# Attention's beginning: modulation as rows that are turned, its second set and the gates behind the first scores, the first stack head by head

## The reference, cut to what matters

```python
mod = (_silu(L0_c) @ L0_wmod).reshape(L0_c.shape[0], 6, 1, -1)      # 8 x 3072 in six parts of 512
sa, ca, ga, sb, cb, gb = (mod[:, 0], ..., mod[:, 5])
ga = (2 * (ga >= 0) - 1) * jnp.maximum(jnp.abs(ga), 0.25)           # gb the same
h = _layernorm(x, axis=-1) * (1 + ca) + sa
x = x + ga * attention(h)            # 16 heads of 32, causal, T = 512, 8 batches
h = _layernorm(x, axis=-1) * (1 + cb) + sb
x = x + gb * mlp(h)                  # 512 -> 1024 -> 1024 -> 512
```

## Time and profile before

| | us |
|---|---|
| median of 3 runs | 1564.84 |
| lowest and highest | 1563.7, 1569.16 |
| the profiled execution | 1568.6 |
| its span, first to last instruction | 1566.8 |
| PE busy in it | 1457.9 (93%) |
| first scores start in it | 55.78 |
| fourth slot (p = 3) starts in it | 94.47 |

### The profile page before, as it was taken

One profiled execution on the slowest core, in us unless ns is written; L12 is line 12 of the kernel. 1 busy time (PEld: TensorE's weight loads), 2 busy tenths in 40 slices (PEclk: granted clock), 3 DMA queues, 4 the chain that ended last, 5 costly groups with the idle time before them and its releaser, 6 DMA issues.

```text
span 1566.8 us, 30447 instructions
## 1 busy us (share of the span) xinstructions
PE 1457.9 (93%) x12112; PEld 1321.2 (84%) x12112; DVE 1110.3 (71%) x1957; ACT 809.5 (52%) x1462; POOL 439.1 (28%) x451
## 2 busy tenths in 40 slices
PE   7989999999999999994699999969999999989998
PEld 6678888788878888873599999969999999989998
DVE  4477877777777777672676676686676666778887
ACT  3156666666676667673355555555243333353331
POOL 2156566656576666672000000000000000000000
PEclk9889999999999999996899999999999999999999
DMA  6534435343434343435344444543665555688885
GB/s 215 161 83 122 97 93 125 86 122 74 123 88 118 94 123 88 95 73 180 122 142 142 141 143 169 214 148 113 238 229 209 209 202 203 219 283 268 284 291 179
DMA packets 126590, 247.16 MB, mean 158 GB/s; under 512 B 13672, under 2 KB 36200, under 8 KB 126448
## 3 DMA queue, kind: packets, MB, share of 16 engines
q1 hardware_dynamic: 122816, 242.57, 49.6%
q10 hardware_dynamic: 3632, 2.64, 0.5%
HBM read 114.58 MB, written 79.72 MB: 124 GB/s over the span
## 4 chain that ended last, share of the span: by engine, by line
PE 42%; DVE 6%; DMA 3%; ACT 2%; issue 1%; DVEq 0%; SPq 0%; ACTq 0%
PE sum_b L2111 11%; PE sum_e L2111 7%; PE sum_a L2111 7%; PE aux L2051 6%; PE sum_b L2107 5%; PE sum_e L2107 3%; PE sum_a L2107 2%; DMA y_dram<-u_c 1%; PE aux L2061 1%; DVE op L1683 1%; DMA gate_mlp_row<-gate_dram 1%; PE aux L2039 1%; DVE w L1819 1%; DVE u_c L1736 1%; DMA x_dram<-x_rows 1%
## 5 line engine op out<-in xcount | busy, mean ns | idle before, releaser
L429 POOL TENSOR_TENSOR prob_lo<-prob,prob_hi 128x512 f16<-128x512 f32 x256 | 296.9, 1164 | 141.6 <-ACT prob L533 141.1
L526 ACT ACTIVATE prob_hi<-key_score 128x512 f16<-128x512 f32 x320 | 191.2, 597 | 132.0 <-PE key_score L824 129.8
L2111 PE MATMUL sum_b<-op,w 128*128 128x256 f32 x1728 | 222.7, 288 | 13.6 <-DVE op L1683 9.8
L2111 PEld LDWEIGHTS sum_b<-op,w 128*128 128x128 f32 x1728 | 216.0, 195 | 16.2 <-issue 11.3
L735 PE MATMUL lin<-h_parts,wqkv 128*128 128x512 f32 x768 | 220.4, 411 | 1.1 <-DVE h_parts L578 1.1
L533 ACT ACTIVATE prob<-key_score 128x512 f32<-128x512 f32 x320 | 190.7, 596 | 0.0
L697 DVE TENSOR_REDUCE row_max<-score 128x1 f32<-128x512 f32 (+2 forms) x384 | 180.6, 499 | 13.5 <-PE score L811 12.7
L735 PEld LDWEIGHTS lin<-h_parts,wqkv 128*128 128x128 f32 x768 | 144.4, 197 | 30.5 <-DVE h_parts L578 2.9
L811 PE MATMUL score<-stack 96*128 96x512 f32 (+3 forms) x512 | 155.6, 365 | 0.0
L2111 PE MATMUL sum_e<-op,w 128*128 128x256 f32 x1152 | 148.1, 286 | 2.7 <-DVE w L1819 2.7
L2111 PE MATMUL sum_a<-op,w 128*128 128x256 f32 x1152 | 145.4, 284 | 2.3 <-issue 2.3
(11 more groups left out here) (153 smaller groups left out, 2574.1 us busy)
## 6 DMA issues: line engine op xcount, KB each, us to landing
stack<-qk_parts SPq DMA_DIRECT2D x384, 128.0 KB, 2.4
late_op_whole<-y_dram SPq DMA_DIRECT2D x40, 512.0 KB, 4.9
y_dram<-u_c SPq DMA_DIRECT2D x32, 512.0 KB, 3.1
blk<-y_dram SPq DMA_DIRECT2D x32, 512.0 KB, 4.5
y_dram<-y_sum SPq DMA_DIRECT2D x24, 512.0 KB, 4.6
x_tiles<-x SPq DMA_DIRECT2D x32, 256.0 KB, 3.7
attn_dram<-o_rows SPq DMA_DIRECT2D x32, 256.0 KB, 2.3
attn_tiles<-attn_dram SPq DMA_DIRECT2D x8, 1024.0 KB, 6.2
```

What stands on the lines that cost most here:

```text
L429: nc.gpsimd.tensor_tensor(prob_lo[:, key[1] % 2, u, :], prob[:, u, :], prob_hi[:, key[1] % 2, u, :], ALU.subtract).then_inc(lo_pool, 1)
L526: nc.scalar.activation(prob_hi[:, q % 2, u, :], bank[:], ACT.Exp, scale=SOFTMAX_SCALE, bias=P_SHIFT)
L2111: mm = nc.tensor.matmul(dst, w[:, wl, c, cols], data[:, dl, c, :], start=begin, stop=end, skip_group_check=again)
```

## The change

1. The modulation is made as rows: `mod_rows(s)` has `silu` as weights (8 columns) and `wm` as 512 moving columns, four matmuls for each of shift and scale, into `key_bank`. ACT copies the rows to SBUF (`take_rows`), and `mod_columns(s)` turns them with four transposes each.
2. `mod_rows(1)` goes to slot 0, step 1, its turning to step 4. `gate_rows` go from slot 0 (steps 2 and 4) to slot 1 (steps 0 and 2). Their parts of `wmod` are loaded by ACT.
3. DVE's `take_gate` is gone. ACT copies the gate rows in slot 1 and POOL makes the gates at the start of slot 2 (`make_gate`, four operations each). PE's wait for the gates becomes one for ACT's copies; ACT's wait for the DMA stays.
4. For the first batch, turns 2 and 3 use the banks of the scores and places in `o_rows`, so the four turns need not wait for one another, and QK 0 and QK 1 are interleaved in PE's list, by rows of `h`.
5. `weights_high` and `weights_low` stand between the turns: one block before, one after turn 1, four after turn 3 (before: three and three).
6. The first stack is issued head by head, with a semaphore for each of the four heads. PE also still waits for `stack_in0`, which SP raises by its whole amount behind its twelfth issue.
7. POOL's constant rows of stacks 2 and 3 move to slot 1.

```diff
-    MOD_STEPS, GATE_STEPS = 2, 10
+    MOD_STEPS, GATE_STEPS = 2, 8
+    def turn_bank_of(n, c):
+        return score_bank[c - 2] if n == 0 and c >= 2 else lin_bank_of((TURN, c))
+    def full_of(n, c):
+        return o[:, c - 2].rearrange("p t n -> p (t n)") if n == 0 and c >= 2 else full[:, c % 2, :]
...
+                if n == 0 and g == 0:
                     for j in range(4):
+                        for block_row in range(3):
+                            load_rows(g, block_row, j, first_stack_in[j])
+                    sp.sem_inc(stack_in[0], 16 * STACK_DMAS)
+                    return
...
-            for step in (1, 2):
-                sp.wait_ge(mod_mm, step)
-                for half in range(2):
-                    load_mod(sp, 2 * step + half)
+            for half in range(2):
+                sp.wait_ge(mod_mm, half + 1)
+                load_mod(sp, 2 + half)
+            for item in before_first():
+                after_item(0, item)
...
+            def make_gate(g):
+                made = 4 * g
+                pool.wait_ge(gate_row, g + 1)
+                if g == 0:
+                    pool.wait_ge(mod_turned, 2)
+                nc.gpsimd.tensor_scalar(sign[:, g], gates[:, g], 0.0, 0.5, ALU.is_ge, ALU.subtract)\
+                    .then_inc(gate_step, 1)
+                pool.wait_ge(gate_step, made + 1)
+                nc.gpsimd.tensor_tensor(gates[:, g], gates[:, g], sign[:, g], ALU.mult).then_inc(gate_step, 1)
+                pool.wait_ge(gate_step, made + 2)
+                nc.gpsimd.tensor_scalar(gates[:, g], gates[:, g], GATE_FLOOR / 2, 4.0, ALU.max, ALU.mult)\
+                    .then_inc(gate_step, 1)
+                pool.wait_ge(gate_step, made + 3)
+                nc.gpsimd.tensor_tensor(gates[:, g], gates[:, g], sign[:, g], ALU.mult).then_inc(gate_step, 1)
             def slot(b, p, first, more):
+                if first and p == 2:
+                    for g in range(2):
+                        make_gate(g)
...
+            def take_rows(s):
+                for j in range(2):
+                    act.wait_ge(mod_mm, 2 * s + j + 1)
+                    nc.scalar.copy((gates, sign)[s][:, j], key_bank[j][0:B, :]).then_inc(mod_row, 1)
+            take_rows(0)
+            weights_high(0)
...
+                    if first and (p, u) == (0, 2):
+                        take_rows(1)
+                        for half in range(2):
+                            load_mod(act, 4 + half)
+                    if first and p == 1 and u in (1, 3):
+                        take_gate(u // 2)
...
             def do_item(n, item):
-                if item[0] == TURN or item[-1] == 0:
-                    place = ORDER.index(unit_of(item))
+                if n == 0 and item in (qk(0)[0], qk(1)[0]):
+                    pe.wait_ge(lin_taken, LIN_CREDITS + item[1] + 1)
+                elif (item[0] == TURN or item[-1] == 0) and not (n == 0 and item[0] == TURN):
                     pe.wait_ge(lin_taken, lin_no(n, unit_of(item)) + 1)
...
-            def mod_columns(s):
+            def mod_rows(s):
                 for j in (SHIFT, SCALE):
                     pe.wait_ge(wm_in[j], 16 * (s + 1))
-                    for block in range(NC_):
-                        at = ((s * 2 + j) * NC_ + block) * B
-                        for c in range(NC_):
-                            mm = nc.tensor.matmul(o_bank[:, at:at + B], wm[:, j, c, block * P:(block + 1) * P],
-                                                  silu[:, c, :], start=(c == 0), stop=(c == NC_ - 1))
-                mm.then_inc(mod_mm, 1)
+                    for c in range(NC_):
+                        mm = nc.tensor.matmul(key_bank[j][0:B, :], silu[:, c, :], wm[:, j, c, :],
+                                              start=(c == 0), stop=(c == NC_ - 1))
+                    mm.then_inc(mod_mm, 1)
...
+                        mm = nc.tensor.transpose(o_bank[:, at:at + B], rows[:, j, block * P:(block + 1) * P],
+                                                 ident[0:B, 0:B])
+            first_items[NC_:3 * NC_] = [item for pair in zip(qk(0), qk(1)) for item in pair]
...
                 if first and p == 2:
-                    pe.wait_ge(gate_step, GATE_STEPS)
-                    pe.wait_ge(ones_ready, 1 + GROUPS)
+                    pe.wait_ge(gate_row, 2)
+                    pe.wait_ge(ones_ready, 3)
...
-                    if first and p == 0 and u in (2, 4):
-                        gate_rows(u // 2 - 1)
+                    if first and (p, u) == (0, 1):
+                        mod_rows(1)
+                    if first and (p, u) == (0, 4):
+                        mod_columns(1)
+                    if first and p == 1 and u in (0, 2):
+                        gate_rows(u // 2)
```

More of the change, by code:

```diff
@@ L229, in attention @@
     stack_in = [mem.sem(f"stack_in{g}") for g in range(GROUPS)]
+    first_stack_in = [mem.sem(f"first_stack_in{j}") for j in range(4)]
     score_done, score_taken, max_hi, turn_done, turn_taken = (
@@ L347, in slot @@
                 for u in range(UNITS):
-                    if first and (p, u) == (1, 3):
+                    if first and (p, u) == (2, 0):
                         sp.wait_ge(gate_step, GATE_STEPS)
@@ L402, in low_part @@
                     pool.wait_ge(lin_taken, LIN_CREDITS + lin_no(n, item) + 1)
-                    nc.gpsimd.tensor_tensor(h[:, 1, c, :], full[:, c % 2, :], f32(h[:, 0, c, :]), ALU.subtract)\
+                    nc.gpsimd.tensor_tensor(h[:, 1, c, :], full_of(n, c), f32(h[:, 0, c, :]), ALU.subtract)\
                         .then_inc(h_low, 1)
@@ L418, in _ @@
             ones(1)
-            pool.wait_ge(w_lo, len(W_ORDER))
-            for g in range(GROUPS // 2, GROUPS):
-                ones(g)
-            pool.wait_ge(ones_ready, 1 + GROUPS)
-            def slot(b, p, first, more):
+            pool.wait_ge(ones_ready, 3)
+            def make_gate(g):
[12 more added lines that the diff above has]
+                nc.gpsimd.tensor_tensor(gates[:, g], gates[:, g], sign[:, g], ALU.mult).then_inc(gate_step, 1)
+            def slot(b, p, first, more):
+                if first and p == 2:
+                    for g in range(2):
+                        make_gate(g)
+                if first and p == 1:
+                    pool.wait_ge(w_lo, len(W_ORDER))
+                    pool.wait_ge(v_split, V_CREDITS + sum(item[0] == V and last_item(item)
+                                                          for item in before_first() + sum(WORK[0], [])))
+                    for g in range(GROUPS // 2, GROUPS):
+                        ones(g)
+                    pool.wait_ge(ones_ready, 1 + GROUPS)
                 for u in range(UNITS):
@@ L491, in after_item @@
                     act.wait_ge(stack_in[(g - 2) % GROUPS], 16 * STACK_DMAS * (n + 1 if g >= 2 else n))
+                    if n == 0 and g == 2:
+                        for j in range(4):
+                            act.wait_ge(first_stack_in[j], 16 * 3)
                 act.wait_ge(lin_done, lin_no(n, unit) + 1)
@@ L646, in _ @@
             normalise(0, range(NT))
-            for k in range(3):
-                weights_low(k)
             take_columns(0)
@@ L651, in _ @@
             take_mod(0)
+            weights_low(0)
             for item in before_first():
                 after_item(0, item)
+                if item == (TURN, 1):
+                    weights_low(1)
                 if item == (TURN, NC_ - 1):
-                    for k in range(3, len(W_ORDER)):
+                    for k in range(2, len(W_ORDER)):
                         weights_low(k)
-            take_columns(1)
             def gather_output(n, q, hh):
@@ L671, in slot @@
                 for u in range(UNITS):
-                    if first and p == 1 and u in (0, 2):
-                        take_gate(u // 2)
+                    if first and (p, u) == (1, 0):
+                        take_columns(1)
                     turned = behind(b, p, 1, first)
@@ L722, in turn @@
                     pe.wait_ge(x_norm, NT * (n + 1))
[L723 removed]
+                bank = turn_bank_of(n, c)
                 for t in range(NT):
@@ L780, in _ @@
             pe.sem_inc(pv_done, PV_CREDITS)
+            pe.wait_ge(pool_step, 8)
             pe.wait_ge(silu_step, 3)
+            mod_rows(0)
             mod_columns(0)
-            pe.wait_ge(pool_step, 8)
-            for item in before_first():
+            first_items = before_first()
+            first_items[NC_:3 * NC_] = [item for pair in zip(qk(0), qk(1)) for item in pair]
+            for item in first_items:
                 do_item(0, item)
-                if item == (QK, 1, NC_ - 1):
-                    pe.wait_ge(mod_taken, MOD_STEPS)
-                    mod_columns(1)
             def masks(b, p, u, key):
```

67 lines of the change are left out of this document (36 added, 31 removed).

## The result

| | before | after |
|---|---|---|
| median, both timed on the same chip (4 runs each) | 1565.44 | 1574.59 |
| lowest and highest after | | 1572.91, 1576.39 |
| the profiled execution and its span | 1568.6, 1566.8 | 1575.26, 1573.4 |
| first scores | 55.78 | 42.70 |
| slot 3 of the first batch | 94.47 | 98.18 |

The changed kernel takes 1.0051 times as long [1.0033, 1.0069]: slower by 0.5%. The forecast was 1562.1, 2.7 us faster, with a range that ended at 1568. Against the kernel before, 9.15 us more were measured by the two medians (8.0 by the ratio) where 2.7 less were expected.

The account below looks back on a forecast made before the run. PE was taken as drawn nearly without gaps, often at half clock. First scores 13.6 us earlier, then step (2, 2) almost 10 us late behind POOL's gates, left a 2.7 us gain: 1564.84 - 2.7 = 1562.1, range 1553.5 to 1568.

Parts of the forecast that it names:

- The path that it named: Slot 2, step (2, 2): PE waits for ACT's exponentials, gates_out and POOL's eight gate operations, opening at 84.0, almost 10 us late.
- mod_rows raise the clock: PE's start: mod_rows(0) runs half clock for 5.6 us, then full, ending at 18.9 instead of 22.73.
- That rival: Rows do not hold the clock: mod_rows run at half speed in the first stage and slot 0; 1572, chance 10%.
- The stage up to the first scores: First batch: QK 0 and 1 start at 24.2, first scores at 42.2, set by SP's twelve stack issues; 13.6 us earlier.
- The wait for the gates' wmod: PE ahead of the gate products: waits for ACT's late loads, bounds 0 and 3 us, taken as 1.0.
- The price of tensor_scalar on POOL: POOL's gate operations: 0.8 us per tensor_scalar, between 0.5 and 1.27, making the eight-operation chain 8.4 us.
- From gates to slot 3: POOL's chain ends at 80.1, gates_out lands at 82.7, step (2, 2) opens at 84.0, slot 3 at 91.8.
- What DVE gives back: Before slot 2, step 2: PE's 5.6 us wait for DVE's row maxima and 5.0 us of half clock go.
- "The rest is shifted as it is.": Behind slot 3 both instruction lists are the same, so the 2.7 us gain carries unchanged to the end.
- All is given back: Rival at step (2, 2): tensor_scalar at 1.27 and landing of 3.5 open it 2.9 us later still; 1565, chance 8%.
- Gates hidden: Rival on POOL: 0.3 us per operation on 8 partitions, slot 3 at 83.2, gain 11, 1553.6; chance 17%.
- the rival that I had set on that side: The slower side: rows of 8-column weights do not hold PE's clock, sum 10.0 us lost, 1572; chance 10%.

Follow-up runs that it names:

- rows_alone: The kernel before with only the modulation made as rows that are turned, slots, gates and stacks unchanged; ratio 0.9987 to the kernel before.
- all_mended: Changed kernel with gates on DVE, gates' wmod loads behind each row copy, no stack_in0 wait in batch 0, two weights_low later; 1554.34 us, ratio 0.9927.
- after_again: The changed kernel, unchanged, profiled a second time; span 1571.0 us.
- after_third: The changed kernel, unchanged, profiled a third time; span 1572.3 us.
- no_gate_math: Changed kernel with POOL's eight gate operations replaced by one signal, so the gates stay raw; ratio 0.9951 to the kernel before.
- gates_on_dve: Changed kernel with the gates made by DVE in three operations each, none on POOL; ratio 0.999 to the kernel before.
- gate_load_early: Changed kernel with ACT issuing each gates' part of wmod behind its own row copy, not behind both; ratio 1.001 to the kernel before.
- before_no_gate_math: The kernel before with each gate's five DVE operations replaced by one copy; ratio 0.9982 to the kernel before.
- gate_copy_ahead: all_mended with the second gate row copied at (1, 2), ahead of the row maxima's DMAs, and the second gate made at (1, 4); ratio 0.9938.
- pool_prices: no_gate_math with twelve extra POOL operations behind the last slot, results unused, to time them; one execution, 1574.51 us with the added work.
- before_third: The kernel before, unchanged, profiled a third time; span 1566.3 us.
- before_again: The kernel before, unchanged, profiled a second time; span 1563.1 us.

## Why the prediction was wrong

The path that it named held, and two prices on it did not: that of tensor_scalar on POOL, which turned the sign, and that of the wait for the gates' `wmod`. The sum put a gain of 13.6 us against a loss of 10.9 between the first scores and slot 3, a difference of two large numbers, and the loss was 16.8.

- **mod_rows raise the clock.** Right: 18.8 for 18.9. The second set took 7.03 for 7.0, at a clock of 1.00. That rival is out; rows_alone shows the same by itself (8.78 and 7.03). No row of the forecast shows that a load of 333 ns in the first 41 us is half clock, as it took for the size of the first QK pair and for the 0.11 us of a transpose; the 330 to 333 ns at 0.50 and 188 at 1.00 in the same trace, above, bear it out.
- **The stage up to the first scores.** Right to half a microsecond: QK 0 starts at 23.8 (24.2), QK 2 at 33.4 (33.6), first scores at 42.7 (42.2), released by SP behind its twelfth issue. The half clock in QK 0 and 1 was 3.4 us (24.9 to 28.3, at 0.50) and not 5.6, but DVE held QK 2 as the forecast said, for 1.84 us instead of 1.0, so the miss did not show. all_mended shows that this hold and `stack_in0` together cost 3.9 us.
- **The wait for the gates' wmod.** Taken at 1.0 of bounds 0 to 3: it was 2.2 in the profiled execution, inside, but by luck. In after_again and after_third it was 3.74 and 3.46, in no_gate_math and gates_on_dve 3.5, so the upper bound was too low. What I left out is what the wait does to the clock: it fell behind it (0.52 from 58.9 to 62.3), and the product took 5.30 for 3.60. Together 3.9 us, not 1.0 (in after_again 3.74 and 2.31, so 6.1). gate_load_early took 4.3 away at slot 3.
- **The price of tensor_scalar on POOL.** This is the step that failed. I took 0.8 and called 1.27 the upper bound, the price of a two-input operation, on the unstated assumption that one input cannot cost more than two. It costs 1.92. Four of them are 4.5 us beyond the forecast, the four tensor_tensor, at 1.25 to 1.28 for 1.2, and the signals 0.3, so the chain lasted 13.2 for 8.4. The row I leaned on was nearer than I let it be: the affine_select at 0.29 for 128 columns gives 1.2 for 512, and I took something off it. Between the engines, on 8x512 of the gates: a tensor_tensor takes 1.25 to 1.28 us on POOL (after) and 0.68 on DVE (before), a tensor_scalar with two operations 1.92 on POOL (after) and 0.39 on DVE (all_mended).
- **From gates to slot 3.** The chain began at 74.35 instead of 71.7, by the 0.5 us of the first scores and the 2.9 more for the wait, of which 2.65 reached it, and its write landed within 1.8 us instead of 2.5. Together: (2, 2) at 84.0 + 2.65 + 4.8 - 0.9 (0.7 of landing, the rest in the exponentials) = 90.5, as measured. From there to slot 3 it took 7.7 us, by the forecast 7.8.
- **What DVE gives back.** The 10.6 us of waits and half clock that before lost to DVE are gone in after, as forecast, but not for the reason given, that DVE's gate operations go: without them before_no_gate_math still waits 3.8 us for row maxima and gains 4.5 at slot 3. With the gates on DVE and PE as late as in after, gates_on_dve has no wait for row maxima; in all_mended, where PE opens slot 1 at 56.3 instead of 66.6, 1.3 us are back, and 3.8 in gate_copy_ahead. So it is argued, though no run tries it alone, that in after PE's own delay hides DVE.
- **"The rest is shifted as it is."** Not quite: 2.6 us more by the repeats, within a scatter of 3.5 us between executions of the same kernel.
- **How much of the miss each step is.** At slot 3, 98.18 came for 91.8, 6.4 us later: 4.8 by the chain's price and 2.65 by its later start, less 1.0. With the chain's price alone put right, the forecast is 1562.1 + 4.8 = 1566.9: slower than before and still inside the range. The rest of the 11.9 us between forecast and measurement is the later start, the 2.6 us behind slot 3 and the scatter of few executions.

By quantity: 16.8 us lost between the first scores and slot 3 = 7.0 + 0.6 for the second set and its turning + 3.9 for wmod + 12.5 idle at (2, 2) + 3.3 for the half clock behind it (half of 6.68) - 5.6 - 5.0 for what before lost to DVE; that is 16.7.

The rivals. "All is given back" named the right place, with a tensor_scalar of 1.27 for 1.92 and a landing of 3.5 for 1.8. "Gates hidden" is refuted by the 1.92 us of the change itself and by pool_prices: 8 partitions cost what 128 do. The slower side came out of the forecast's own chain, which I had bounded from above by a row of another kind of operation, and not out of the rival that I had set on that side.

## What to carry to other kernels

Here the price of an operation that no row showed was not bounded by a row of another kind on the same engine (1.92 us against 1.27): one like it should be measured first, when a chain of them decides the sign. Nor was the work that moved to an idle engine free, since ACT waited 15.3 us for the DMA behind it: POOL's eight operations took 13.2 us, and slot 3 came 13.0 us sooner without them, while DVE made the same gates in 3.5 us. The short wait of PE had a second price, the clock behind it (0.52 from 58.9 to 62.3): 2.2 us of waiting cost 3.9. A wait that one execution shows is one draw: the same wait was 3.5 to 3.7 us in the next ones.

## What the runs showed of the hardware

- POOL, float32: a tensor_scalar of 512 columns takes 1.92 us with two operations and 1.49 with one, a tensor_tensor 1.03 to 1.28 (after, pool_prices); for the first and the last of these 8 or 128 partitions make no difference (pool_prices). DVE takes 0.38 to 0.40 for the same two-operation tensor_scalar on 8 partitions (all_mended, gates_on_dve).
- The same wait of 1.7 us in front of the same instruction is followed by half clock in some executions and by full clock in others (0.51 in before, 1.00 in before_third, from 194.9 to 197.7 us). Between slot 3 and the MLP's stage that goes with a spread of 3.5 us in each kernel.
- From the MLP's first load to the end the thirteen executions in the two tables (each kernel's profiled one and the repeats) took 841.4 to 846.7 us. Five took 841.4 to 842.7, with 57 to 61 us of that stretch at half clock, six took 844.4 to 846.7, with 63 to 69 us; no_gate_math and gate_load_early took 843.7 and 843.8 with 55 us, so the clock is not all of it. That kernels which reach this stage earlier are slower in it does not follow: before_again and before_third reached it at 721.1 both and took 842.0 and 845.1. No run tries the cause.
